# A fused convolution and mixture-of-experts kernel: forty pages ahead of the last scatters, the second centring before the norm, three last groups page by page

## The reference

```python
x = x + conv_ref(ln_c(x), ...)          # sign, conv, bn, relu, sign, conv, bn, + residual, relu
t = to_tokens(x)                        # 16 x 1024 tokens of 64 channels
n = ln_t(t)
probs = softmax(n @ gate_w + gate_b)    # 16 experts
top_probs, top_idx = top_k(probs, 2);  top_probs /= sum(top_probs)
h = silu(n @ w1[e]) * (n @ w2[e])       # hidden width 128, for every expert e
y = sum over the two chosen e of top_probs[e] * (h @ w3[e])
x = from_tokens(t + y)
```

## Time and profile before

| | us |
|---|---|
| median of 3 runs | 505.14 |
| the runs | 503.07 to 505.5 |
| the profiled execution, its own time | 508.51 |
| its span, first to last instruction | 506.6 |
| PE busy in the span | 450.2 (89%) |
| DVE busy | 439.2 (87%) |
| ACT busy | 408.6 (81%) |
| POOL busy | 296.1 (58%) |

### The profile page before, as it was taken

One profiled execution on the slowest core, in us unless ns is written; L12 is line 12 of the kernel. 1 busy time (PEld: TensorE's weight loads), 2 busy tenths in 40 slices (PEclk: granted clock), 3 DMA queues, 4 the chain that ended last, 5 costly groups with the idle time before them and its releaser, 6 DMA issues.

```text
span 506.6 us, 14224 instructions
## 1 busy us (share of the span) xinstructions
PE 450.2 (89%) x4186; PEld 385.8 (76%) x4186; DVE 439.2 (87%) x1245; ACT 408.6 (81%) x946; POOL 296.1 (58%) x380
## 2 busy tenths in 40 slices
PE   7999989999997628999849999999999999999971
PEld 6676777777774516889748898889999898898961
DVE  3677798988989988999919999999999999999982
ACT  4687888888876304999929999999999999999960
POOL 3200008777777777777777666666555555556562
PEclk9899889999997656999979999999999999999996
DMA  6884011022000014330034223243342525410054
GB/s 165 144 343 172 0 43 63 30 70 72 29 31 29 29 49 89 86 70 32 28 77 84 59 52 60 59 103 68 82 117 51 135 62 137 100 38 18 21 172 166
DMA packets 62664, 40.97 MB, mean 81 GB/s; under 512 B 50003, under 2 KB 54318, under 8 KB 62080
## 3 DMA queue, kind: packets, MB, share of 16 engines
q1 hardware_dynamic: 52784, 29.30, 23.4%
q0 software_dynamic: 8800, 8.94, 5.3%
q10 hardware_dynamic: 1008, 1.84, 1.0%
HBM read 21.46 MB, written 19.19 MB: 80 GB/s over the span
## 4 chain that ended last, share of the span: by engine, by line
PE 47%; DVE 31%; ACT 9%; issue 7%; DMA 3%; POOL 1%; SPq 1%; POOLq 0%; DVEq 0%; ACTq 0%
PE up L979 10%; PE up L981 9%; PE turn L992 6%; PE up L809 4%; DVE xs_lo L1524 4%; ACT xc L709 4%; PE lines L1011 4%; DVE hidden L1600 3%; PE small L825 3%; PE small L960 3%; DVE hidden L1605 2%; PE up L784 2%; PE lines L1013 2%; DVE sq L1600 1%; PE small L1022 1%
## 5 line engine op out<-in xcount | busy, mean ns | idle before, releaser
L534 POOL DMA_INDIRECT results<-result,page_in x147 | 156.4, 1064 | 94.8 <-ACT xc L709 51.0
L513 POOL DMA_INDIRECT pages<-payload,slot_int x128 | 131.3, 1025 | 98.3 <-DVE slot_int L1425 60.5
L979 PE MATMUL up<-up_w,xs_hi 128*128 x588 | 139.0, 276 | 7.8 <-DVE xs_lo L1524 6.7
L981 PE MATMUL up<-up_w,xs_lo 128*128 x588 | 138.4, 275 | 0.0
L709 ACT ACTIVATE xc<-up,back_scales 128x512 f32<-128x512 f32 x147 | 107.8, 733 | 12.6 <-PE up L981 10.5
L1610 DVE TENSOR_TENSOR hidden_lo<-turn,hidden_hi 128x512 f16<-128x512 f32 x98 | 67.4, 688 | 9.7 <-ACT hidden_hi L722 8.7
L979 PEld LDWEIGHTS up<-up_w,xs_hi 128*128 128x128 f16 x588 | 58.0, 99 | 19.0 <-issue 12.2
L722 ACT ACTIVATE hidden_hi<-turn 128x512 f16<-128x512 f32 x98 | 65.1, 664 | 8.6 <-PE turn L992 8.6
L1600 DVE SCALAR_TENSOR_TENSOR hidden<-up,page_in,xc 128x128 f32<-128x128 f32 x196 | 59.4, 346 | 7.0 <-ACT xc L709 6.3
L981 PEld LDWEIGHTS up<-up_w,xs_lo 128*128 128x128 f16 x588 | 58.1, 99 | 5.5
L992 PE MATMUL turn<-ident,hidden 128*128 128x128 f32 x392 | 59.3, 274 | 0.0
(11 more groups left out here) (265 smaller groups left out, 967.0 us busy)
## 6 DMA issues: line engine op xcount, KB each, us to landing
pages<-x SPq DMA_DIRECT2D x4, 1332.0 KB, 11.3
page_in<-pages SPq DMA_DIRECT2D x147, 36.0 KB
page_in<-pages SPq DMA_DIRECT2D x147, 32.0 KB
x_in<-in_x SPq DMA_DIRECT2D x7, 512.0 KB, 3.5
out<-up_raw SPq DMA_DIRECT2D x5, 512.0 KB, 3.1
results<-result,page_in POOLq DMA_INDIRECT x147
up_raw<-in_L_ffn_w SPq DMA_DIRECT2D x4, 512.0 KB, 7.9
pages<-payload,slot_int POOLq DMA_INDIRECT x128, 2.2
```

Of the source, the lines that this page charges most:

```text
L513: pool.indirect_dma_start(out=pages, out_offset=bass.IndirectOffsetOnAxis(ap=slot_int[q % PAYLOADS][:, t:t + 1], axis=0), in_=payload[q % ...
L534: pool.indirect_dma_start(out=results, out_offset=bass.IndirectOffsetOnAxis(ap=page_in[g % LOADS][:, k, D + AT_TOKEN:D + AT_TOKEN + 1].bit ...
L979: pe.matmul(target, xs_hi[g % 2][:, k * P:(k + 1) * P], weights[:, bass.ds(e * 2, 2 * HID)], start=True, stop=False)
L981: last = pe.matmul(target, xs_lo[g % 2][:, k * P:(k + 1) * P], weights[:, bass.ds(e * 2, 2 * HID)], start=False, stop=True)
```

## The change

- `SOON` goes from 32 to 40: forty seats are taken by full pages, and the load that waits for all scatters is that of group 10.
- In the last pair's scatter loop, every second scatter is followed by the write of one result (`put_result`): results 0 to 7 (`MIXED`) go out among the 16 scatters, the others after them as before. These eight have no wait for `silu_done`.
- `groups_of_pair` takes the forty seats into account (pair 0: 15 groups instead of 14), and pair 0's return steps move from pages 75 and 79 to pages 83 and 87.
- PE's order in a round: both halves of `center2` stand ahead of `norm`, where the second half stood behind it.
- The down weights' low part (`make_low(2)`) moves on DVE from round index 9 to 5, ahead of `x_norm`.
- Groups 34, 35 and 36 are handled page by page (`LAST` = 136). Pages 136 to 140 use the bank `lines`, each waiting for the addition of the page before; from page 141 the banks `lines` and `small` alternate as before (`APART` = 140).

```diff
-    SOON = 32
+    SOON = 40
+    MIXED = 8
...
-            return min(GROUPS, -(-(TILES * (q + 1) + LINES - 1 + ahead) // BY))
+            return min(GROUPS, -(-max(TILES * (q + 1) + LINES - 1 + ahead, SOON + LINES) // BY))
...
-        back_step = {TILES * q + 75 + BY * c: (q, c) for q in range(EARLY) for c in range(CH)}
+        back_step = {TILES * q + (75 if q else 83) + BY * c: (q, c) for q in range(EARLY) for c in range(CH)}
...
-        last_down = {BY * g + pages_of(g) + LAG: g for g in range(GROUPS - 2)}
-        LAST = BY * (GROUPS - 2)
+        last_down = {BY * g + pages_of(g) + LAG: g for g in range(GROUPS - 3)}
+        LAST = BY * (GROUPS - 3)
+        APART = BY * (GROUPS - 2)
         def last_bank(n):
-            return (lines, small)[(n - LAST) % 2]
+            return small if n > APART and (n - APART) % 2 else lines
         def last_ready(n):
-            return GROUPS - 2 + n - LAST + 1
+            return GROUPS - 3 + n - LAST + 1
...
                         in_=payload[q % PAYLOADS][:, t, :], in_offset=None)\
                         .then_inc(scattered[q % PAYLOADS], 16)
-            for q in range(PAIRS):
-                scatter(q)
+                    if q == PAIRS - 1 and t % 2 == 1:
+                        put_result(t // 2)
...
-            for n in range(PAGES):
+            def put_result(n):
                 g, k = n // BY, n % BY
-                pool.wait_ge(silu_done, min(PAGES, result_page(n)))
                 if n >= LAST:
                     pool.wait_ge(result_ready, last_ready(n))
                 elif k == 0:
...
+            for q in range(PAIRS):
+                scatter(q)
+            for n in range(MIXED, PAGES):
+                pool.wait_ge(silu_done, min(PAGES, result_page(n)))
+                put_result(n)
...
                 if k == 0:
-                    act.wait_ge(result_ready, g - 1 if g == GROUPS - 2 else last_ready(LAST) - 1)
+                    act.wait_ge(result_ready, g - 1 if g < GROUPS - 1 else last_ready(APART - 1))
...
                 if 0 <= s < PAIRS:
-                    center2(0, s)
+                    for c in range(CH):
+                        center2(c, s)
                 if a < PAIRS:
                     for c in range(CH):
                         norm(c, a)
...
-                if 0 <= s < PAIRS:
-                    center2(1, s)
...
                 if n >= LAST:
                     bank, at = last_bank(n), 0
-                    pe.wait_ge(result_ready, max(GROUPS - 2, last_ready(n - 2)))
-                    if n == LAST + 1:
+                    if n == LAST:
+                        pe.wait_ge(low_read, g)
+                    else:
+                        pe.wait_ge(result_ready, last_ready(n - 1 if n <= APART else n - 2))
+                    if n == APART + 1:
                         pe.wait_ge(back_read, CH * EARLY)
...
-                if t in (3, 4):
+                if t in (3, 4, 5):
                     make_low(t - 3)
...
-                if t == PAIRS + 1:
-                    make_low(2)
```

## The result

The changed kernel takes 498.83 us (median of 4 runs, 496.59 to 499.56), the kernel before beside it 504.42 (503.07 to 505.5). The ratio is 0.9866, with an interval of [0.983, 0.9902]. The forecast was 499.6. A second set gave 499.73 against 506.48: 0.9874, [0.9834, 0.9914].

A forecast was written before the change was run, and what follows sets the result against it. The prediction took POOL's queue of scatters and results, which delays page loads, and POOL's gap at the end as the bounds; 3.6 + 0 + 0 + 1.9 = 5.5 us gained gives 499.6 us, range 496.8 to 502.8.

The forecast's parts named there:

- The stop at group 8 and its cause: Page loop: POOL's order of scatters and results sets PE's 7.99 us stop before group 8; the change removes it.
- The stop at group 9 and its slow restart: Page loop: a 4.4 us stop at group 9 replaces 8.0, slow restart of 1.73 kept; gain 3.6 us (2.6 to 4.0).
- the bound given for no slow restart: Page loop, group 9: the gain would be 5.3 us if PE did not restart at a lowered clock.
- rival B: Group 9's stop short enough to keep the clock up, or first scatter earlier: 7.2 to 8.1 gained, 497.5 us; chance 0.17.
- rival A: The forecast itself: a shorter stop at group 9 and a tail without POOL's gap, 499.6 us (498 to 501.5); chance 0.50.
- The second centring: Early rounds: round 3 takes what round 2 gives; 0 for the first scatter, bounds 0.9 us earlier and 1.7 later.
- the bound for round 2 alone: First scatter up to 0.9 us earlier if only round 2's saving from the swapped centring counts.
- The low part: DVE, round 6: page loop starts up to 0.9 us earlier, swallowed by group 9's wait; scatter hold of 0.9 moves along: 0.
- The rule cited from the Trainium skill: A VectorE operation with two SBUF inputs and a GpSimd operation reading SBUF exclude each other for a whole instruction.
- The tail: Last three groups page by page: POOL's results run as one row, the last ending earlier; gain 1.9 us (0.8 to 2.3).
- The bank's loss: Tail: pages 136 to 140 share one PSUM bank, each waiting for the previous page's addition; taken as 0.3 us.
- The sum: Whole kernel: 3.6 + 0 + 0 + 1.9 = 5.5 us gained, giving 499.6 us from the median of 505.14.

The follow-up runs named there:

- seats_alone: The kernel before with only the forty seats (and pair 0's later return steps), no results among the scatters: 505.13 us against 505.06, ratio 1.0001.
- mixing_alone: The kernel before with only the eight results among the last scatters (and pair 0's later return steps), thirty-two seats: 511.76 us, ratio 1.0106.
- early_no_centring: The whole change without the centring edit, with one result behind every scatter of the last pair (sixteen) and forty-eight seats: 494.7 us, ratio 0.9785.
- all_again: The whole change run once more, as yardstick and second profile: 499.73 us against 506.48 for the kernel before, ratio 0.9874.
- tail_only: The kernel before with only the last three groups handled page by page: 505.54 us against 505.77, ratio 0.9994.
- centring_only: The kernel before with only both centrings put ahead of the norm's turn: 504.26 us against 505.77, ratio 0.997.
- no_tail: The whole change but with two groups page by page as before, not three: 499.88 us against 505.06 for the kernel before, ratio 0.9897.
- no_low: The whole change but with the down weights' low part back at its old place: 499.08 us against 505.06 for the kernel before, ratio 0.9893.
- low_only: The kernel before with only the down weights' low part moved to round index 5: 503.49 us against 505.77, ratio 0.997.
- mixed_only: The kernel before with only the forty seats and eight results among the scatters (and pair 0's later return steps): 502.22 us against 505.77, ratio 0.9933.

## Why the prediction was right, point by point

**The stop at group 8 and its cause: right.** POOL's order set it, as forecast: result 7 at 179.0 (forecast: 179.3), group 9 used 8.4 later (8.4; 8.0 to 9.7 in the six traces with a stop there). seats_alone, mixing_alone and early_no_centring move the dates at which the loads may leave, and the stop moves with them as POOL's order says.

**The stop at group 9 and its slow restart: mis-sized.** The step that failed is PE's date for group 9, taken as the old 251.76 + 7.57. The forecast said that an earlier or later page loop "only changes how long PE stands there", and left the loop's start out of the sum. But the clock went with the length of the stop: it stayed at 1.00 in the five traces with stops up to 1.92 and fell to 0.50 in the eight with stops of 5.32 and more. The page loop started 1.1 to 2.7 us later behind the first scatter, PE wanted the group at 185.0 and 186.5 instead of 183.3, the stop was 1.92 and 0.84 instead of 4.4, and the 1.73 that the forecast kept for the restart was not paid. At group 10 the gain is 200.5 - 194.9 = 5.6 (all_again: 6.0), where 3.6 was taken; the bound given for no slow restart, 5.3, was the right value. No trace has a stop of 4.4, so whether the restart would have been slow behind the stop that was forecast is not shown. Both conditions of rival B came true (for the first scatter see below), in a kernel whose time is rival A's.

**The second centring: taken as 0 for the first scatter.** Reckoned from the end of PE's first variance, the first scatter comes after 60.7 to 61.1 us in the six traces with the centring ahead and after 61.4 to 62.3 in the eight without: 0.9 earlier on the mean. That is the size of the bound for round 2 alone, but the way there was not the one forecast. In tail_only and centring_only, whose first variances end alike (13.13), the variance that is at 29.84 in the earlier trace rows starts at 29.53 and 28.81, the one at 46.85 starts at 48.18 and 46.67, the next at 58.61 and 58.51, and the one behind that at 68.42 and 67.49. So in this pair round 3 did not take back what round 2 gave; the lead grew to 1.5, went to 0.1 and came back to 0.9, and why is open. What the edit does in later rounds was left out, since only the first scatter's date was to matter. It moved the start of the page loop, and with it the restart.

**The low part: 0, right.** The hold did not move along whole, though: at the new place a scatter took 1.39 to 1.46 in five traces, a hold of 0.4 to 0.5, and in the changed kernel and no_tail none was held, where it had been 0.9 (and 0.3 in no_low). In the twelve traces with a held scatter it ends 0.82 to 0.84 us after the operation does, so how much of the hold is paid depends on where in the operation a scatter starts, which the forecast did not work out. The rule cited from the Trainium skill ("SBUF — State Buffer", section "SBUF: two separate sides") agrees with these twelve. By the order of the starts it would also have put the changed kernel's scatter behind the end of the low part; here it ran through at 0.96 inside the 1.31 of the operation, so the trace does not agree in this place.

**The tail: mis-sized.** 1.9 was forecast, 0.4 to 0.8 measured. The bank's loss was 0.7, not 0.3, and the rest is a term the sum did not have: behind a last result that comes 1.41 earlier on POOL, the way to the end became 11.25 - 10.38 = 0.87 longer, nearly all of it in the last result's DMA.

**The sum.** 5.5 was forecast. The terms measured, 5.6 to 6.0 at group 10, 0.9 at the first scatter and some 0.6 in the tail, make 7.1 to 7.5; the ratios of the two sets give 6.8 and 6.4, their medians 5.6 and 6.75. Two terms were too low and one too high, so that the time came out within 1 us of the forecast is in part luck. The sign for the reader to look for, a first scatter within 1 us of 76.02, was badly chosen: the start-up alone moves it by up to 2.5 us from trace to trace (PE's first variance ends between 11.19 and 13.73; the first scatter is at 72.91 in low_only, whose first rounds are those of before).

## What to carry to other kernels

When a buffer's load has two waits, work out the date of each: an edit that moves one of them is worth nothing, or less, until the other is moved too. Price a stop together with what the clock does behind it, since an edit "swallowed by a wait" can still pay or cost by making that wait short enough to keep the clock (here up to 1.92 us), or long enough to lose it (here from 5.32). And when the stop itself is removed, look again at the edits that only paid because of it: here the centring, which helps with eight early results and, by the traces, no longer with sixteen.

## What the runs showed of the hardware

Behind stops of 0.61, 0.84 (twice), 1.65 and 1.92 us PE's granted clock stayed at 1.00 (2.4 GHz) and the next group came after 7.57 to 7.67; behind the eight stops of 5.32 to 12.76 it was 0.50 (1.2 GHz) and the next group came after 9.30 to 10.09. The loss did not grow with the stop: 9.36 behind 12.76, 10.09 behind 6.19. No run here has a stop between 1.92 and 5.32.

The same DVE operation beside POOL's scatters held one of them by 0.9 us in six traces (old place), by 0.3 in one (no_low, old place), by 0.4 to 0.5 in five (new place) and not at all in two (the changed kernel and no_tail). The twelve held scatters start 0.25 to 0.83 us after the operation's start and end 0.82 to 0.84 us after its end. In the two without a hold the scatter starts 0.05 or 0.06 us after the operation's start and takes 0.96 or 0.95, and the operation takes 1.31 where it takes 1.27 or 1.28 in the twelve.

The last result's DMA took 2.10 or 2.11 us in six of the kernels without the third page-by-page group and 2.9 to 3.0 in five with it; mixed_only (2.58), early_no_centring (2.58) and no_low (2.34) lie between. Why is open; it was not tried.
